# Expert stage rewritten: weights by DMA, products on GpSimd, down projections in three f32r passes, no loops

## The reference, cut to what matters

```
x = x + attention(layernorm(x))        # 16 heads of 8, causal, window 128
h = layernorm(x)                       # 8192 tokens x 128
scores = sigmoid(h @ gate_w.T)         # 16 experts; 2 of 4 groups, then 4 experts by score + bias
w = 2.5 * chosen scores / their sum    # 4 non-zero weights per token, 12 zeros
y = sum over experts e of w[e] * (silu(h @ G[e].T) * (h @ U[e].T)) @ D[e].T     # 64 inner columns
x = x + y + (silu(h @ Gs.T) * (h @ Us.T)) @ Ds.T                                # shared expert
```

## Time and profile before

| | us |
|---|---|
| median of 3 runs (lowest, highest) | 808.34 (807.64, 811.28) |
| the profiled execution's own time | 805.08 |
| its span, first to last instruction | 803.3 |
| PE busy | 745.7 (93%) |
| DVE busy | 599.4 (75%) |
| ACT busy | 370.6 (46%) |
| POOL busy | 174.2 (22%) |
| first matmul of the expert stage, and its last store issued | 403.45, 800.67 |

### The profile page before, as it was taken

The page is one execution under the profiler, slowest core; times in us unless marked ns, Lnnn a source line. Parts: engine busy times, 40 slices in busy tenths (PEclk is TensorE's granted clock), DMA queues, the critical chain, the costliest instruction groups (busy, mean ns, idle before and its releaser), DMA issues. The chain is left out here.

```text
span 803.3 us, 23092 instructions
## 1 busy us (share of the span) xinstructions
PE 745.7 (93%) x8627; PEld 483.5 (60%) x8627; DVE 599.4 (75%) x1870; ACT 370.6 (46%) x745; POOL 174.2 (22%) x285
## 2 busy tenths in 40 slices
PE   3598999999999999999699999999999999999997
PEld 2355666666666666665466566666656656666664
DVE  6777888787888888885477678776778767787764
ACT  2166677566666666674533322333223332233321
POOL 6522111122212222221022022120221202222000
PEclk9599999999999999996889999999999999999999
DMA  2136232322332333331011101111001111010000
GB/s 56 55 93 168 80 96 74 95 68 72 95 97 95 96 97 95 96 95 31 1 67 39 40 7 32 39 39 39 17 22 39 39 39 31 8 39 26 26 14 13
DMA packets 47410, 45.64 MB, mean 57 GB/s; under 512 B 10193, under 2 KB 38113, under 8 KB 47329
## 3 DMA queue, kind: packets, MB, share of 16 engines
q1 hardware_dynamic: 47328, 44.50, 18.1%
HBM read 27.44 MB, written 17.04 MB: 55 GB/s over the span
## 5 line engine op out<-in xcount | busy, mean ns | idle before, releaser
L913 DVE TENSOR_REDUCE chunkmax<-ps_max 128x16 f32<-128x512 f32 (+1 forms) x256 | 155.2, 647 | 37.6 <-PE ps_max L1303 37.6
L799 ACT ACTIVATE spare<-ps_max 128x512 f32<-128x512 f32 x144 | 86.0, 597 | 210.1 <-PE ps_max L1574 170.9
L715 ACT ACTIVATE probs<-ps_sc 128x512 f32<-128x512 f32 x256 | 139.0, 596 | 52.4 <-PE ps_sc L1340 51.3
L1590 PE MATMUL ps_c<-spare,wd 128*128 128x512 f32 x256 | 125.4, 592 | 0.0
L1129 DVE TENSOR_TENSOR spare<-spare,ps_sc 128x512 f32<-128x512 f32 x128 | 87.2, 681 | 20.5 <-ACT spare L799 11.7
L1137 DVE TENSOR_TENSOR spare<-spare,ps_att 128x512 f32<-128x512 f32 x128 | 87.2, 681 | 10.0 <-PE ps_att L1582 6.1
L1572 PE MATMUL ps_max<-xh,whigh 128*128 128x512 f32 x144 | 78.5, 545 | 0.0
L529 POOL TENSOR_TENSOR veps<-meanvar,eps 128x4 f32<-128x4 f32 x32 | 7.6, 238 | 317.1 <-DVE meanvar L877 317.1
L1364 PE MATMUL ps_sc<-qkstack 32*64 32x192 f16 (+2 forms) x2048 | 64.7, 234 | 11.0 <-issue 4.8
L1390 PE MATMUL ps_att<-probs,vdiag 128*32 128x192 f32 (+1 forms) x1536 | 71.4, 321 | 0.0
L1322 PE MATMUL ps_max<-hl,qdiag 32*128 32x160 f16 (+4 forms) x1024 | 50.7, 219 | 17.2 <-DVE chunkmax L913 10.3
(11 more groups left out here) (166 smaller groups left out, 1334.2 us busy)
## 6 DMA issues: line engine op xcount, KB each, us to landing
qkstack<-qk_scratch SPq DMA_DIRECT2D x48, 256.0 KB, 3.5
qk_scratch<-hl SPq DMA_DIRECT2D x32, 256.0 KB, 3.5
xin<-in_L_attn_x_dram SPq DMA_DIRECT2D x16, 256.0 KB, 3.2
x_scratch<-x SPq DMA_DIRECT2D x16, 256.0 KB, 2.2
xin<-x_scratch SPq DMA_DIRECT2D x16, 256.0 KB, 2.9
xres<-x_scratch SPq DMA_DIRECT2D x16, 256.0 KB, 2.7
out_dram<-result SPq DMA_DIRECT2D x16, 256.0 KB, 2.2
max_scratch<-rowmaxT SPq DMA_DIRECT2D x32, 8.0 KB, 1.4
```

Source lines behind the costliest of these rows:

```text
L715: nc.scalar.activation(dst[:, :], ps_sc[s][:, 0:dst.shape[1]], ACT.Exp, scale=SCALE).then_inc(probs_ready, 1)
L799: nc.scalar.activation(silu[slot][rows, :], ps_max[slot][rows, :], ACT.Silu).then_inc(silu_ready, 1)
L913: nc.vector.tensor_reduce(chunkmax[:, 2 * pair + m, at:at + CHUNKS[h]], ps_max[m][:, 0:BANK_COLS[h]].rearrange("p (n k) -> p n k", k=KB), ...
L1590: last = mm(ps_c[:, :], wd[:, p, :], inter[p % 3][:, :], start=(p == 0), stop=False)
```

## The change

Weights reach the 64 partitions of an expert by DMA: POOL makes the weights (one product, `scale_weight`), PE transposes them as float32, ACT copies them out, SP stores 16 rows of 512 to scratch and loads them back, each row repeated onto 64 partitions (two DMAs of 1 MB a block), into `spread`, which takes the memory of the attention stage's stacks. `spread_weight` and the bf16 parts are gone. `weigh` moves from DVE to POOL. Each product is split: ACT copies `inter` to a high f32r tile, and inter minus high gives the low tile, on POOL for p = 0, 2, 4, 6 and on DVE for p = 1, 3, 5, 7, 8. `down` becomes three f32r matmuls. Routing runs two blocks ahead; the routing of blocks 0 and 1 and the transposes of x1 blocks 1 and 2 move into `last`. PE's `down` runs on across the block's end, and the result of a block is added in the middle of the next one. The three banks of transposed down weights are split by DVE too, as the others are. The hardware loops go; all waits are on constants. silu, gated, inter and yT use the attention stage's `probs` tiles.

```diff
+        spread = [t[:, :].rearrange("p (n t) -> p n t", t=TOK) for t in stacks]
+        wd = sb("wd", [P, 2, NP, E], F32R)
+        WEIGHT_BANKS.insert(4, (("x", 1), TOK))
+        WEIGHT_BANKS.append((("x", 2), TOK))
+        N_SPLIT = len(WEIGHT_BANKS)
+        WEIGHT_BANKS += [(("weight",), TOK)]
+        LOW_ON_POOL = (0, 2, 4, 6)
@@ SP
+            def store_weight(d):
+                sp.wait_ge(weightT_ready, d + 1)
+                after(sp, spread_loaded[d % 2], 32 * (d // 2))
+                sp.dma_start(wt_d[d % 2], weightT[d % 2][:, :]).then_inc(weight_stored[d % 2], 16)
+            def load_spread(d):
+                if d < 2:
+                    sp.wait_ge(pv_done, 6 * (STEPS - 1 + d))
+                else:
+                    sp.wait_ge(inter_ready, NP * (d - 1))
+                sp.wait_ge(weight_stored[d % 2], 16 * (d // 2 + 1))
+                src = wt_d[d % 2].rearrange("(n a) t -> a n t", a=2)
+                for a in range(2):
+                    sp.dma_start(spread[d % 2][I * a:I * a + I, :, :], src[a].partition_broadcast(I)
+                                 ).then_inc(spread_loaded[d % 2], 16)
@@ POOL
-            def split_weights(k):
...
+            def weigh(d, p):
+                if p == 0:
+                    pool.wait_ge(spread_loaded[d % 2], 32 * (d // 2 + 1))
+                pool.wait_ge(gated_ready, (NP + 1) * d + p + 1)
+                after(pool, down_done, (NP + 1) * d + p - 2)
+                nc.gpsimd.tensor_tensor(inter[p % 3], gated[p % 2], spread[d % 2][:, p, :], ALU.mult
+                                        ).then_inc(inter_ready, 1)
+            def low_inter(d, p):
+                if d < 0 or p not in LOW_ON_POOL:
+                    return
+                pool.wait_ge(inter_high_ready, (NP + 1) * d + p + 1)
+                nc.gpsimd.tensor_tensor(inter_low[p % 3][:, :], inter[p % 3], inter_high[p % 3][:, :].bitcast(FP32),
+                                        ALU.subtract).then_inc(inter_low_pool, 1)
+            for d in range(STEPS):
+                for p in range(NP):
+                    weigh(d, p)
+                    low_inter(d, p - 1)
+                    if p == 1 and more:
+                        inverse_deviation(STEPS + d + 3)
+                    if p == 2 and more:
+                        centre(STEPS + d + 3)
+                    if p == 3 and more:
+                        normalise(STEPS + d + 3)
+                scale_weight(d + 2)
@@ ACT
+            def high_inter(d, p):
...
+                nc.scalar.copy(inter_high[p % 3][rows, :], inter[p % 3][rows, :]).then_inc(inter_high_ready, 1)
@@ DVE, one block
-                gate(k, 3)
-                sum_groups(k)
-                weigh(k, 3)
-                compare_groups(k)
+                gate(d, 3)
+                low_inter(d, 2)
+                if route:
+                    choices(d + 2)
+                    sum_pairs(d + 2)
+                gate(d, 4)
+                low_inter(d, 3)
+                if d > 0:
+                    add_y(d - 1)
...
@@ PE
-                    last = mm(ps_c[:, :], wd[:, p, :], inter[p % 3][:, :], start=(p == 0), stop=False)
+                    parts = [(wd[:, 0, p, :], high[:, :]), (wd[:, 0, p, :], low[:, :]), (wd[:, 1, p, :], high[:, :])]
+            for d in range(STEPS):
+                for p in range(NP + 1):
+                    up(d, p)
+                    n = (NP + 1) * d + p - 3
+                    if n >= 0:
+                        down(n // (NP + 1), n % (NP + 1))
+                    if p == 1:
+                        route(d + 2)
+                    if p == 2:
+                        transpose_weights(d + 1)
+                    if p == 4 and d > 0:
+                        transpose_y(d - 1)
+                    if p == 7:
+                        transpose_x1(d + 3)
```

More of the change, by code:

```diff
@@ L341, in low_of @@
                 return wlow[:, 2 * NP, :]
-            return wrt[:, 1, :]
[L344 to L352, removed]
+            if what[0] == "x":
+                return xl[what[1]][:, :]
+            if what[0] == "down":
+                return wd[:, 1, what[1]:what[1] + 4, :].rearrange("p n k -> p (n k)")
+            if what[0] == "sh_down":
+                return wds[:, 1, :]
+            return wrt[:, 1, :]
         def after(engine, semaphore, value):
@@ L1198, in _ @@
             last(STEPS - 1)
-            def ffn_first(k):
-                low_x(k.next())
-            def ffn_step(k):
-                more = not (k.j is None and k.c + 1 >= STEPS)
-                gate(k, 0)
-                weigh(k, 0)
-                sum_logits(k)
-                clip(k)
+            for d in range(STEPS):
+                route, more = d + 2 < STEPS, d + 3 < STEPS
+                if d > 0:
+                    low_x(d + 2)
+                gate(d, 0)
+                low_inter(d - 1, NP)
@@ L1210, in ffn_step @@
                 if more:
[L1211 to L1214 removed]
+                    tile_statistics(STEPS + d + 3, 0)
+                gate(d, 1)
+                low_inter(d, 0)
                 if more:
[L1216 to L1221 removed]
@@ L1239, in ffn_step @@
-                gate(k, 7)
-                weigh(k, 7)
-                gate_shared(k)
-                add_y(k)
-                if more:
-                    low_x(k.next())
-            def ffn_last(k):
-                for p in range(NP):
-                    gate(k, p)
-                    weigh(k, p)
-                gate_shared(k)
-                add_y(k)
-            steps(dve, ffn_first, ffn_step, ffn_last)
+                    tile_statistics(STEPS + d + 3, 1)
+                    join_statistics(STEPS + d + 3)
@@ L1520, in transpose_weight @@
                         last = nc.tensor.transpose(bank[:, t * P:(t + 1) * P], wgu_raw[:, what[1] + t, :], ident[:, :])
+                elif what[0] == "x":
+                    pe.wait_ge(xhat_ready, STEPS + 1 + what[1])
+                    for t in range(NT):
+                        last = nc.tensor.transpose(bank[:, t * P:(t + 1) * P], xhat[:, t, :], ident[:, :])
+                elif what[0] == "weight":
+                    pe.wait_ge(weight_ready, 1)
+                    for t in range(NT):
+                        last = nc.tensor.transpose(bank[0:NE, t * P:(t + 1) * P], weight[:, t, :], ident[:, :])
+                    last.then_inc(weight_tr_done, 1)
+                    pe.wait_ge(weight_tr_done, 1)
+                    pe.sem_inc(fw_done, 1)
+                    return
                 elif what[0] == "sh":
@@ new lines, in up @@
+            def up(d, p):
+                n = (NP + 1) * d + p
+                after(pe, silu_ready, n - 1)
+                after(pe, gated_ready, n - 1)
+                if p == 0 and d >= 3:
+                    pe.wait_ge(xl_ready, d - 1)
+                slot = n % 2
+                for q, bank in ((p, ps_max), (NP + p, ps_sc)) if p < NP else ((2 * NP, ps_max),):
+                    mm(bank[slot][:, :], whigh[:, q, :], xh[d % 3][:, :], start=True, stop=False)
+                    mm(bank[slot][:, :], whigh[:, q, :], xl[d % 3][:, :], start=False, stop=False)
+                    last = mm(bank[slot][:, :], wlow[:, q, :], xh[d % 3][:, :], start=False, stop=True)
```

662 lines of the change are left out of this document (322 added, 340 removed).

## The result

The changed kernel takes 815.85 us (median of 10 runs, 812.36 to 819.45) beside 808.17 us before (805.58 to 811.28, 10 runs): ratio 1.0095, interval 1.0069 to 1.0122. It is slower, as forecast, but by 7.7 us and not by 25. The profiled execution took 815.79 us, span 814.0.

What follows compares the result with a forecast made beforehand. It took DVE and POOL blocking each other's SBUF reads as the bound, 26.2 us per full block. From 805.1, start +5.5, blocks +15.9, end +3 made 829.5; 3.3 to the median gave 833. Own range 815 to 858, with rivals 770 to 858.

Steps and rivals of the forecast that it cites:

- Direction and kind of mechanism: Expert stage: DVE steps reading SBUF wait for whole POOL instructions, making the kernel slower; port blocking, chance 0.59.
- the five large ones: DVE's five new two-input subtractions per block: each charged a whole POOL product, 1.3 us; small routing steps charged nothing.
- The walk through the block: Longest chain through one expert block, POOL product 1 to the next block's: 26.2 us, 22.4 without blocking.
- Its four parts: Block walk to the ends of POOL products 3, 5, 7 and the next block's 1: 7.3, 5.9, 5.3, 7.7 us.
- Blocks without routing: Two blocks of the expert stage without routing: 22.5 us each.
- the end: End of the expert stage: `down` waits for product, copy and subtraction instead of product alone, +3 us.
- The work of each engine: Per expert block after the change: PE 21.0 us, DVE 16.6, ACT 12.6, POOL 20.4.
- The start: Start of the expert stage: first `up` about 405, first POOL product waits for spread until near 410; some 5.5 us late.
- The loop: ACT's table load in every second block goes with the hardware loop: worth up to 0.6 us per block.
- No blocking that matters: Rival at DVE's five subtractions: POOL and PE nearly full, 22.4 us per block, 774 us in all; chance 0.31.
- Blocking of the small steps as well: Slower end of the forecast: DVE's small routing steps wait for POOL too, block 27.4 us instead of 26.2.
- The signs named: Port blocking would show subtractions over 1 us, POOL above 75%, PE holes ahead of `down`, results 25 us or more apart.

Runs made afterwards that it cites:

- e2: e1 with twelve idle POOL products per block that nobody reads or waits for: 817.77 us, ratio 1.0193 to the kernel before.
- e4: The changed kernel with one operand of each small DVE routing step in PSUM and one small copy added: 768.85 us, ratio 0.956 to the kernel before.
- e1: The kernel before with its hardware loops written out, nothing else changed: 792.48 us beside 804.92, ratio 0.9851.
- e10: e8 with two of the nine subtractions on POOL (pairs 0 and 4) instead of four: 764.99 us, ratio 0.9477 to the kernel before.
- e7: e4 with the spread weights loaded in two halves, a semaphore each: 767.95 us, ratio 0.9549 to the kernel before.
- e6: e4 with ACT making the experts' scores ahead of the copy of inter 2: 771.11 us, ratio 0.958 to the kernel before.
- e8: e4 with both the edits of e6 and e7: 767.03 us, ratio 0.9528 to the kernel before.
- e3: e1 with eight idle POOL memsets of 1.8 us per block, which read nothing: 797.91 us, ratio 0.9917 to the kernel before.
- e11: e8 with one of the nine subtractions on POOL (pair 2), eight on DVE: 803.49 us, ratio 0.9945 to the kernel before.

## Why the prediction was right or wrong

**Direction and kind of mechanism: right.** An instruction of DVE's that reads through what POOL reads waits until POOL's is over; e2 shows it with little else changed, and e4 shows that taking it away from the small steps gives 43 us (from 1.0095 to 0.956 of the kernel before's 808). The size was wrong, 25 us forecast and 7.7 measured, and so was the place.

**Which instructions pay: wrong, and this is the step that failed.** The prediction put a whole POOL product on "the five large ones, and nothing for the small ones", and charged the large ones' locks to the length of every block. The traces show the reverse. Per block the small steps gained 0.87 (score), 0.98 (choice), 0.70 (pair_sums), 0.66 (needles), 1.06 (chosen), 0.71 (total) and 0.29 (masked), each the mean after less the mean in e1 (`masked`: L1097, 0.518 against 0.226): 5.3 us. The four large subtractions gained 0.2 each and the shared one nothing (0.677): 0.8 us. POOL's eight products gained 0.16 each, 1.3 us:

```profile
L629 POOL TENSOR_TENSOR probs<-probs,stacks 128x512 f32<-128x512 f32 x98 | 141.1, 1445 | 61.2 <-DVE probs L1144 58.4 <-PE ps_c L1641 2.7
```

(after, lines grouped by form, 480 to 790 us). That is 2.1 us in place of 6.4, a whole product for each of five; the walk itself carried 3.8 of them, 26.2 against 22.4 without blocking. Three of the steps that pay stood on no list of mine: needles and total, with one input, and the masking at L1097, with two. The reason, read from the timelines and tested by no run, is the order of work. A subtraction waits for ACT's copy, that waits for a POOL product, and by then POOL is at its next instruction or waits for a gate, so what is left of the lock is short (the subtractions of pairs 1, 3, 5 and 7 take about 1.10, 0.68, 0.92 and 0.78 in a full block, 0.42 over the undisturbed 0.68 at most), or DVE is first and POOL pays 0.4 (1.69 against 1.29). The small steps wait for nothing of POOL's and stand in rows, so that each meets a fresh POOL instruction.

**The walk through the block: 26.2 forecast, 25.98 measured, right by cancellation, which is luck.** Its four parts, from the ends of POOL's products in one block of the trace: 6.4 (forecast 7.3), 6.6 (5.9), 5.7 (5.3), 7.2 (7.7). The first is shorter, since low 1 did not hold POOL and products without a wait start 1.25 us apart, not the 1.37 taken from the earlier trace rows. The second and third are longer by the blocked score, choice, pair_sums and needles. With the small steps at their price and the rest unchanged, the walk gave 27.4. It had counted 0.6 us of POOL's time for a lock at each of five subtractions.

**Blocks without routing: here the error shows.** They have no small steps. Forecast 22.5 each; the intervals are 18.4 and 19.3: 7.4 us of the miss. The large subtractions stand there too, beside the same products. DVE's line by form, 770 to 806 us, and the window of the first of the two:

```profile
L1160 DVE TENSOR_TENSOR inter_low<-probs,inter_high 128x512 fp32r<-128x512 f32 x7 | 7.8, 1111 | 0.1
```

```profile
767.90:786.20 18.30, 18.21 (x81) 14.04 (x81) 11.26 (x15) 10.51 (x18) 16.32 (x12) 1.00 0.49 108
```

So here the subtractions do wait, 0.4 us each, more than in the full blocks, and the block is 3 to 4 us shorter than forecast all the same: DVE is busy only 11.3 of 18.3 us and PE 18.2. The lock is real and does not set the length of these blocks; PE's matmuls do. To charge it to the block was the mistake.

**The account of the miss.** Forecast 829.5 for the profiled execution, measured 815.8. Of the 13.7 the last two blocks are 7.4, the twelve full ones 12 x 0.22 = 2.6, the one without normalisation 0.6, start and first block together 1.0 (+7.0 forecast to the mark, 5.5 and 1.5 for its block; +6.0 measured), the end 1.9 (+3 against +1.1), and 0.2 is rounding. The other 3.3 up to 833 are the step from the profiled execution to the median, which the kernel after does not have (815.79 and 815.85).

**The work of each engine: right.** DVE 16.6 forecast; 16.6 + 5.3 + 0.8 = 22.7, and 22.9 measured, of which some 6 us are waits. POOL 20.4, measured 20.7. ACT 12.6, measured 12.1. PE 21.0, measured 22.1 with holes inside, and e10 runs a block in 22.5 with PE 95% busy, so 21.4 is its work. DVE's busy time is a poor sign of load here, since waiting for the port counts as busy.

**The start: right in size, off in place.** The first `up` was at 400.6 and not 405, the first product at 409.4 (forecast 410), after 5.3 us of waiting for spread. e7 shows that this wait was the dear part, and the `up` ahead of it was not. The +6.0 is good to 2 us or so: the weight product that starts the chain stands at 402.4 to 404.9 in the traces of kernels with the same attention stage (e4, e6, e7, e8).

**The loop: about as priced.** Up to 0.6 us per block forecast; the blocks of e1 show 9.8 us in fifteen, 0.65 each (12.4 in the medians, interval 1.1 to 1.9%). It sat within PE's term, which did not bound the full blocks, so the forecast did not feel it.

**The rivals.** "No blocking that matters" (22.4 a block, 774) is what e4 builds: 22.74 and 769. Its arithmetic was right, its condition false. Blocking of the small steps as well was listed as the slower end; it is real, but in place of the large ones, not on top.

**The signs named.** Results 25 us or more apart and POOL at 75% of a block (80%): seen. Subtractions over 1 us: not seen in the full blocks (0.886), only in the last two (1.11). By its own text the forecast is wrong "if the subtractions are not longer beside POOL": in the full blocks they are by 0.2.

## What to carry to other kernels

Before moving work to POOL, list every DVE instruction that reads two SBUF tiles, or copies or scales from SBUF to SBUF, whatever its size: a step of 0.2 us costs what is left of the POOL instruction that is running, here up to 1.1 us, and rows of small steps cost most. Price each by what releases it: here the steps released by POOL's own results met little of the next lock and the independent ones nearly all of it. Then ask whether the wait lies on the block's path: in the last two blocks it did not. Then put one operand in PSUM, where there is room, before moving anything back; it was worth 43 us here, against 3 to 4 for the best of the other edits, which is not clear of the intervals.

## What the runs showed of the hardware beside that

- A POOL memset leaves DVE's two-input steps alone (0.225) and stalls tensor_scalar from SBUF to SBUF (0.195 to 1.58), so the read side and the write side lock apart. One such wait can stand in the records of several instructions: `below`, `over`, two statistics and a product all end within 0.04 us of one another in e3, so their excess over the usual length must not be added up.
- POOL's 128x512 products and the instructions behind them, with no wait between, start 1.25 us apart (572.36 and 573.61), less than the 1.29 shown for one.
- With one subtraction on POOL (pair 2) instead of two (pairs 0 and 4) the block is 2.8 us longer (e10 to e11). Two small steps then fall beside POOL's instructions, which is 2.0 of it; that this is the cause is read from the trace and no run isolates it.
- The hardware loops cost 9.8 us in the blocks of a kernel that had PE busy without a hole; a table load of 1.28 us in every second block, 7.7 us in all, is the larger part of it.
